# A state-space scan on one Trainium2 core: pairs of steps summed on GpSimd before TensorE turns them

## What is computed

```python
def step(h, inp):
    dtt, ut, bt, ct = inp                       # dtt, ut: (B, K, D); bt, ct: (B, K, N)
    dA = jnp.exp(dtt[..., None] * A)
    h = h * dA + (dtt * ut)[..., None] * bt[:, :, None, :]
    y = jnp.einsum('bkdn,bkn->bkd', h, ct)      # the sum over the N = 16 states
    return (h, y)
...
ys = ys + Ds.reshape(K, D)[None, :, :, None] * u
y = _cross_merge(ys, H, W)                      # the sum over the K = 4 directions
```

## Time and profile before

| | us |
|---|---|
| median of 3 runs | 11385.86 |
| lowest and highest | 11383.32, 11387.95 |
| the profiled execution, its own time | 11378.4 |
| its span from first to last instruction | 11376.6 |
| PE busy | 8954.9 (79%) |
| DVE busy | 7592.8 (67%) |
| ACT busy | 3900.4 (34%) |
| POOL busy | 3956.4 (35%) |
| runs 4 to 9 of image 2 (counted from 0) | 721.2 |
| runs 4 to 9 of the last image | 391.9 |

### The profile page before, as it was taken

One profiled execution on the slowest core, in us unless ns is written; L12 is line 12 of the kernel. 1 busy time (PEld: TensorE's weight loads), 2 busy tenths in 40 slices (PEclk: granted clock), 3 DMA queues, 4 the chain that ended last, 5 costly groups with the idle time before them and its releaser, 6 DMA issues.

```text
span 11376.6 us, 106333 instructions
## 1 busy us (share of the span) xinstructions
PE 8954.9 (79%) x36120; PEld 4204.5 (37%) x36120; DVE 7592.8 (67%) x5637; ACT 3900.4 (34%) x4474; POOL 3956.4 (35%) x1678
## 2 busy tenths in 40 slices
PE   6985888588886888768896788858898688877556
PEld 2223333343334433344333433334333443334433
DVE  3127667866677667776668666686677766687892
ACT  1113344333333333432443334333333323343331
POOL 0004333433334333442334333343234423343560
PEclk8665888788886898778886888868898789878657
DMA  1006444744457444664447534474445744466782
GB/s 34 4 19 207 154 144 166 245 172 143 140 179 241 156 141 152 216 200 149 148 148 244 193 129 156 163 244 164 136 148 190 225 155 141 153 225 195 246 267 65
DMA packets 717974, 1876.29 MB, mean 165 GB/s; under 512 B 258897, under 2 KB 274641, under 8 KB 717265
## 3 DMA queue, kind: packets, MB, share of 16 engines
q1 hardware_dynamic: 717392, 1869.00, 49.4%
HBM read 1772.03 MB, written 71.04 MB: 162 GB/s over the span
## 4 chain that ended last, share of the span: by engine, by line
PE 57%; DVE 25%; issue 7%; ACT 5%; DMA 2%; DVEq 2%; SPq 1%; ACTq 1%; POOL 0%; POOLq 0%
DVE R L1630 11%; PE ps L902 9%; PE ps L875 8%; PE ps L748 8%; PE ps L855 7%; PE ps L984 7%; DVE ps L1620 6%; PE ps L886 4%; ACT R L1174 3%; PE ps L1069 3%; DVE nmx L1560 2%; PE ps L1052 2%; PE ps L891 1%; PE ps L957 1%; PE ps L981 1%
## 5 line engine op out<-in xcount | busy, mean ns | idle before, releaser
L1345 POOL TENSOR_TENSOR R<-R 128x1024 f32<-128x1024 f32 x1536 | 3659.8, 2383 | 5546.8 <-DVE ps L1620 5546.8
L1630 DVE TENSOR_TENSOR_SCAN R<-R,ps 128x1024 f32<-128x1024 f32 x1536 | 3508.1, 2284 | 440.1 <-ACT R L1233 334.1
L1233 ACT ACTIVATE R<-R,negA 128x1024 f32<-128x1024 f32 x1536 | 1749.9, 1143 | 2946.0 <-DVE R L1630 2908.6
L984 PE MATMUL ps<-ident,R 128*128 128x128 f32 x12288 | 2068.0, 327 | 588.1 <-POOL R L1345 547.5
L984 PEld LDWEIGHTS ps<-ident,R 128*128 128x128 f32 x12288 | 1746.1, 171 | 1512.1 <-POOL R L1345 753.3
L1620 DVE TENSOR_TENSOR ps<-R 128x1024 f32<-128x1024 f32 x1536 | 1993.1, 1298 | 109.3 <-DVE R L1630 4.7
L1560 DVE TENSOR_REDUCE nmx<-ps 128x2 f32<-128x1024 f32 x768 | 936.4, 1219 | 850.1 <-PE ps L855 843.9
L902 PE MATMUL ps<-R 128*128 128x512 f32 x2400 | 1258.6, 648 | 0.0
L1174 ACT ACTIVATE R<-ps 128x1024 f32<-128x1024 f32 x768 | 785.8, 1023 | 1325.6 <-PE ps L875 1325.6
L875 PE MATMUL ps<-R 33*128 33x512 f32 x3072 | 1048.0, 765 | 173.9 <-ACT R L1174 88.4
L855 PE MATMUL ps<-R 32*128 32x512 f32 x3072 | 939.4, 690 | 198.9 <-DVE nmx L1560 164.6
(11 more groups left out here) (154 smaller groups left out, 5749.7 us busy)
## 6 DMA issues: line engine op xcount, KB each, us to landing
R<-bc_scratch SPq DMA_DIRECT2D x3072, 512.0 KB, 4.7
R<-in_x SPq DMA_DIRECT2D x72, 512.0 KB, 6.8
out<-R SPq DMA_DIRECT2D x72, 512.0 KB, 5.2
R<-shift_scratch SPq DMA_DIRECT2D x48, 640.0 KB, 7.4
R<-R SPq DMA_DIRECT2D x192, 128.0 KB
R<-out SPq DMA_DIRECT2D x48, 512.0 KB, 8.4
R<-in_w_qkvo SPq DMA_DIRECT2D x32, 576.0 KB, 6.7
rows_scratch<-R SPq DMA_DIRECT2D x24, 512.0 KB, 7.3
```

The lines of the kernel that those rows point to most:

```text
L984: mm = pe.matmul(ps[:, 4 + b // 4, (b % 4) * P:(b % 4 + 1) * P], state[i % HELD][:, b * P:(b + 1) * P], ident[:, :], start=fresh and i % G ...
L1233: act.activation(decay[i % len(decay)], dt[:, c, :], ACT.Exp, scale=negA[:, col:col + 1]).then_inc(a_sb.h, 1)
L1345: pool.tensor_tensor(state[i % HELD], state[i % HELD], rows_c[slot], ALU.mult).then_inc(hc_sb.h, 1)
L1630: v.tensor_tensor_scan(h, a, b, 0.0, ALU.mult, ALU.add).then_inc(h_sb.h, 1)
```

## The change

In runs 4 to 9, 96 of the 192 steps of an image, two neighbouring steps become a pair. For the odd step of a pair POOL, after its product, adds the product of the even step to it (a new instruction of the same shape, after a drain of POOL). PE turns only this sum: the eight transposes of each even step in these runs fall away, those of the odd step wait for the sum. A run there begins on PE at its second step, and the wait for the copied-out sum and the reload move there with it. DVE's wait for a free state buffer is split in two: the buffer of an even step is free when the pair is summed, that of an odd step when it is turned. ACT's copy at a run's end counts turns instead of steps. The time table that orders the other events is the same.

```diff
+PAIRED = frozenset(range(4, 10))
...
+def paired(i):
+    return i // GN_ in PAIRED
...
+def pairs(i):
+    return sum(paired(j) for j in range(1, i, 2))
...
+def turns(i):
+    return sum(not paired(j) or j % 2 for j in range(i))
...
         for kind, lag, late in (("h", 1, 0.91), ("z", LAG, 0.92)):
+            if kind == "z" and paired((u - lag) % STEPS1) and (u - lag) % 2 == 0:
+                continue
...
-                    pe.wait_ge(hc_sb.h, hc_sb.at(img, i + 1))
-                    if i % GN_ == 0:
+                    begins = i % GN_ == int(paired(i))
+                    if paired(i):
+                        pe.wait_ge(pair_sb.h, pair_sb.at(img, pairs(i + 1)))
+                    else:
+                        pe.wait_ge(hc_sb.h, hc_sb.at(img, i + 1))
+                    if begins:
...
                     pool.tensor_tensor(state[i % HELD], state[i % HELD], rows_c[slot], ALU.mult).then_inc(hc_sb.h, 1)
+                    if paired(i) and i % 2:
+                        pool.drain()
+                        pool.tensor_tensor(state[i % HELD], state[i % HELD], state[(i - 1) % HELD], ALU.add)\
+                            .then_inc(pair_sb.h, 1)
...
-                    if i >= HELD or not first:
-                        v.wait_ge(y_ps.h, y_ps.at(img, i - HELD + 1))
+                    of, j = (img, i - HELD) if i >= HELD else (img - 1, i - HELD + STEPS1)
+                    if (i >= HELD or not first) and paired(j) and j % 2 == 0:
+                        v.wait_ge(pair_sb.h, pair_sb.at(of, pairs(j + 2)))
+                    elif i >= HELD or not first:
+                        v.wait_ge(y_ps.h, y_ps.at(of, turns(j + 1)))
```

More of the change, by code:

```diff
@@ L505, in build @@
         hc_sb = sem("state_times_c_ready", STEPS1)
-        y_ps = sem("y_transposed", STEPS1)
+        pair_sb = sem("pair_summed", len(PAIRED) * GN_ // 2)
+        y_ps = sem("y_transposed", turns(STEPS1))
         y_sb = sem("y_sum_ready", STEPS1 // GN_)
@@ L971, in scan @@
                     fresh = i < NC * GN_
-                    pe.wait_ge(hc_sb.h, hc_sb.at(img, i + 1))
-                    if i % GN_ == 0:
+                    begins = i % GN_ == int(paired(i))
[4 more added lines that the diff above has]
+                    if begins:
                         if 0 <= i // GN_ - (STEPS1 // 2 // GN_ - NC + 1) < NC:
                             pe.wait_ge(mg_y.h, mg_y.at(img, i // GN_ - (STEPS1 // 2 // GN_ - NC)))
-                        elif i or not first:
+                        elif i >= GN_ or not first:
                             pe.wait_ge(y_sb.h, y_sb.at(img, i // GN_))
@@ L985, in scan @@
                                        state[i % HELD][:, b * P:(b + 1) * P], ident[:, :],
-                                       start=fresh and i % GN_ == 0 and b % 4 == 0, stop=i % GN_ == GN_ - 1,
+                                       start=fresh and begins and b % 4 == 0, stop=i % GN_ == GN_ - 1,
                                        is_transpose=True, skip_group_check=True)
@@ L1219, in scan @@
                 if kind == "y":
-                    act.wait_ge(y_ps.h, y_ps.at(img, GN_ * (u + 1)))
+                    act.wait_ge(y_ps.h, y_ps.at(img, turns(GN_ * (u + 1))))
                     if u == 0 and not first:
```

## The result

| | before | after |
|---|---|---|
| median, us | 11384.59 (4 runs) | 11485.35 (4 runs) |
| lowest and highest | 11382.62, 11387.95 | 11470.89, 11499.10 |
| ratio after to before, 95% interval | | 1.0088, 1.0071 to 1.0106 |
| the profiled execution, its span | 11376.6 | 11497.1 |
| mean granted clock of PE | 0.813 | 0.782 |

The kernel became slower by 101 us, where 136 us of gain were forecast. Of the 120.5 us between the two profiled spans, 82.1 lie in runs 4 to 9 of the last image, 15.7 in those of the other seven, and 22.7 outside, where run 10 of images 1 to 6 takes 3.6 us more in each (110.6 in place of 107.0). So the last image did what was forecast, and the seven images gave nothing. (In images 1 to 6 the window takes between 713.5 and 723.5 us after, 721.3 to 721.6 before.)

What follows compares the result with a forecast made beforehand. PE was taken as nearest bound in middle images, DVE in the last. 7 x (35 - 4) = 217 us gained, 85 lost, net 132, so 11250 us predicted, 1.2% less; 8 in 10 range 11145 to 11400.

Steps and rivals of the forecast that it cites:

- The local saving: PE, runs 4 to 9: each missing turn is worth 0.87 us on the chain, 0.82 us in a softmax stretch.
- The worry about DVE's reduction: Maximum stretches: without the turn, scores could begin 0.9 us sooner, but DVE's reduction leaves only 0.1 us of room.
- Nothing new can bind there: I count these turns in full.: Softmax stretches: about 22 of 48 missing turns per image count in full, 22 x 0.87 = 19 us.
- the 70% for the maximum stretches: Of the remaining 26 turns per image, 70% come through: 0.7 x 26 x 0.87 = 16 us.
- the whole 35 us per image: Gain from missing turns in a middle image, softmax 19 plus maximum 16 us; ends 19 and 42.
- The clock: Rival: fewer turns could raise or lower PE's clock; 0.03 more gives 11100 us; 0.13 shared with cheaper holding.
- Another granted clock in the same window: Sign of a wrong prediction: PE's granted clock in runs 4 to 9 differs from before; no size given.
- The last image: DVE's drives are held 1.85 us per pair, 48 pairs, all on the path: 85 us lost (62 to 106).
- The additions in the middle images: Held drives cost nothing in softmax stretches; in maximum stretches 4 us per image on the path (1 to 12).
- No waits of the turns for POOL: PE's turns find room for a sum 2.4 us later, since three steps lie between product and turn.
- The one that ended slower: Rival: held drives are on the path in middle images too, 24 of 48 pairs at 1.85 us: 11534; slower 0.13.
- the fourth, with its other sign: Rival on PE's clock, as a fall: fewer turns could open gaps and lower it; no time given for that.

Runs made afterwards that it cites:

- run 10: Not a follow-up: the run of scan steps behind step 159 in an image, where nothing was changed; images 1 to 6 took 110.6 us in place of 107.0.
- experiments 1: The changed kernel without POOL's addition and its drain; the even turns of runs 4 to 9 stay out, output incomplete: 11476.69 us, ratio 1.0087.
- 4: The changed kernel with pairs in images 0 to 6 only and eight transposes of a zero tile for each missing turn: 11376.68 us, ratio 0.9991.
- 9: The changed kernel, pairs in images 0 to 6 only, one narrow zero matmul per missing turn (eight zero transposes at a run's first step): 11295.49 us, ratio 0.9927.
- experiment 12: The kernel before, all turns, no additions, plus one narrow zero matmul behind even steps' turns (not a run's first), images 0 to 6: 11559.56 us, ratio 1.0161.

## Why the prediction was wrong, point by point

- **What bounds the kernel.** Right for the last image (DVE), right in part for the middle: PE is the nearest bound, but the prediction read PE's busy time as an amount of work. It is work divided by the clock.
- **The local saving.** Right where the clock holds: 0.75 us at the place shown above. In maximum stretch 1 of image 2 the seven missing turns gave 5.6 us, 0.80 each, but the clock rose there from 0.90 to 0.92; the prediction took 0.87 and counted 70% of it. The worry about DVE's reduction was needless there: PE's matmuls L874 waited for it 6.3 us in all, where L855 waited 5.8 before.
- **"Nothing new can bind there: I count these turns in full."** This is the step that failed, and with it the 70% for the maximum stretches: the whole 35 us per image were priced at an unchanged clock. In the mean of images 1 to 6 the three softmax stretches (up to step 160) gave 4.3 us where 19 were forecast, the three maximum stretches 0.9 where 16 less 4 for the additions were; the pieces between them took 4.3 us more. In softmax stretch 1 it failed in two ways. At the turn of step 82 the scores waited for ACT's copy before, and the turn cost nothing; the row with the 0.33 us wait was there to be read. And the stretch's clock fell, to 0.75. In the place of the 7.0 us forecast for its eight turns (8 x 0.87) stood a loss of 7.2. In maximum stretch 2 of image 2 the clock fell too, from 0.94 to 0.87, and with seven turns fewer it took 3.2 us longer.
- **The clock.** It stood as a rival with an open sign ("raise it, or ... lower it"), but a time was worked out only for the rise, and the range had no place for a fall. Its own formula had the size: the window went from 0.88 to 0.83, so 0.05/0.88 x 640 = 36 us per image, against the 35 us counted as gain. ("Another granted clock in the same window" stood among the signs that would show it wrong; that is the sign that came.) The two cancel, and the windows of images 1 to 6 are indeed the same as before, within 1 us each in the mean. That the fall is the cause is shown by experiments 1 (turns away, nothing added: slower than before by 89 us with the last image at its old time, and one and the same run 10 at two clocks, 17 us apart), 4 (zero turns: clock and time of before) and 9 (a cheaper filler: clock 0.823, 97 us faster than with holes). The Trainium skill's rule in "TensorE: Matmul & The Clock Gate", section "Part 4: PE-mode transpose", by which fewer transposes would leave the clock as it is or better, is contradicted here: removing them lowered it from 0.88 to 0.83, and transposes of zeros brought back 0.89.
- **The last image.** Right: 85 us forecast, 82.1 measured in the window, 93 and 87 in the medians of the two pairs of kernels that differ by it. The place in the order was right too (drive first, addition late, next drive held for 3.08 us), and 1.85 us per pair was near: 82.1/48 = 1.71.
- **The additions in the middle images.** 4 us per image were charged. In experiment 4 the whole window took 1.7 us less than before, with 4.7 us more in maximum stretch 2 and between the stretches and a somewhat higher clock elsewhere; so the term is neither confirmed nor refuted at its size. That DVE's held drives vanish in its waits was right: in the changed kernel DVE waited 30.3 us at the divisions (L1594) in image 2, where the earlier trace rows have 50.2.
- **No waits of the turns for POOL.** Right: over runs 4 to 9 of image 2, PE's weight loads waited for L1371 twice, 1.7 us together:

```profile
PEld ps L1007 <- POOL R L1371: 1.7, 2, 0.8
```

- **The rivals.** The one that ended slower got the sign, by the wrong mechanism: it put the held drives on the path, and experiments 1 and 4 exclude that. What happened was the fourth, with its other sign.
- **Outside the window.** The prediction ended its sum at step 159. Run 10 of images 1 to 6, where nothing was changed, took some 3.6 us longer in each, at a clock of 0.82 in place of 0.84; in experiment 1 it took up to 129.3 us, at 0.70.

What stays open: why the clock was back after 3.4 us behind one 2.99 us wait and after 41.0 behind the same wait with fewer turns around it. The runs show which work ahead of it goes with which, not the rule by which the chip decides. So the size of a fall could not have been worked out from the rows of before, only that it had to have a price. Filling only those holes that lie ahead of a fall was not tried.

## What to carry to other kernels

Work taken from PE in a stretch where it takes turns with ACT or DVE is a gain only if the granted clock holds: read the clock of each stretch before, give a fall a price of its own, (fall/clock) x busy PE, and a place in the range. Look at each place where the removed work stood: if the next instruction waited for another engine there, the work was free, and its hole may cost. Where a hole must remain, one cheap matmul that waits for nothing can be worth more than it takes (here 97 us in 11392). It was worth it in place of a hole; on top of a full PE it cost 178 us (experiment 12). Whether it would have paid without the zero transposes at the runs' first steps was not tried.

## What the runs showed of the hardware that was not expected

- The granted clock of the execution went with what stood in the holes, although it was zeros: 0.787 with nothing, 0.805 with four transposes, 0.814 with eight, 0.823 with one narrow matmul.
- PE's busy time can rise when work is removed: 97.40 to 106.25 us in softmax stretch 1, with 70 instructions fewer.
- Four matmuls of 128x32 by 512 columns took 1.06 us into four different groups of 32 PSUM partitions (L905) and 3.62 us into one and the same, both at the higher clock; a single one took 1.04.
- PE stayed at the lower level for 41.0 us while it was busy for 39.45 of them.
- The same 374 matmuls of run 10 took 129.3 us in one image and 112.0 in the next of the same execution, at clocks of 0.70 and 0.80.
- A GpSimd addition that starts 0.15 us behind a drive of DVE takes 3.28 us instead of about 2.35; the mean of all 384 at L1371 was 2829 ns.
